# A gated four-layer transformer block on one core: the waits of an instruction written in another order

## The reference

```python
def reference(x, ctx, mask, g_xattn, g_ffn, ...):
    # layer 0: differential attention, 32 heads of 8; then 3 cycles of a coupling network
    x = x + tanh(g_xattn[0]) * L0_xattn(ln(x), ctx, ...)
    x = x + tanh(g_ffn[0])   * L0_ffn(ln(x), ...)
    # layer 1: 8 heads of 64, 512 keys, masked; then 2 shared + 8 routed experts, top 2, silu
    x = x + tanh(g_xattn[1]) * L1_xattn(ctx, ln(x), mask, ...)
    x = x + tanh(g_ffn[1])   * L1_ffn(ln(x), ...)
    # layer 2: 16 heads of 16; then attention of 16 heads of 8 and 8 experts, top 2, gelu
    x = x + tanh(g_xattn[2]) * L2_xattn(ln(x), ctx, ctx, ...)
    x = x + tanh(g_ffn[2])   * L2_ffn(ln(x), ...)
    # layer 3: one head of 256; then relu, 1024 hidden, weights and activations rounded to 8 bits
    x = x + tanh(g_xattn[3]) * L3_xattn(ln(x), ctx, ctx, ...)
    x = x + tanh(g_ffn[3])   * L3_ffn(ln(x), ...)
    return x
```

## Time and profile before

| what | value |
|---|---|
| median of three runs | 4452.66 us (4442.44 to 4463.31) |
| the profiled execution's own time | 4455.96 us |
| its span, first to last instruction | 4454.2 us |
| PE busy | 4098.3 us, 92% |
| PEld busy | 3191.7 us, 72% |
| DVE busy | 2944.5 us, 66% |
| ACT busy | 2054.1 us, 46% |
| mean granted TensorE clock | 0.953 of full speed |

### The profile page before, as it was taken

How to read it: one execution, slowest core, us unless ns; L and a number is a source line. 1 busy time by engine, 2 the same in 40 slices (tenths; PEclk the granted TensorE clock), 3 DMA queues, 4 the chain that set the end, 5 groups by cost and what they waited for, 6 DMA issues and landing times.

```text
span 4454.2 us, 73894 instructions
## 1 busy us (share of the span) xinstructions
PE 4098.3 (92%) x28256; PEld 3191.7 (72%) x28256; DVE 2944.5 (66%) x7812; ACT 2054.1 (46%) x3424; POOL 91.8 (2%) x180
## 2 busy tenths in 40 slices
PE   7898998989989899898999989899899998989988
PEld 4675876758767596675966759667696676867768
DVE  7666686676766767666675666757667576675754
ACT  4534455443553535535355352653535534355332
POOL 0000000000000000000000000000000000000000
PEclk8998999999999899998999999999999998999989
DMA  2010510103101030010300103001130011200012
GB/s 100 1 46 11 199 58 1 46 29 124 39 12 43 20 133 30 15 41 29 124 30 15 41 30 124 29 15 41 38 115 29 15 41 48 105 29 15 31 67 90
DMA packets 51769, 228.06 MB, mean 51 GB/s; under 512 B 4832, under 2 KB 21216, under 8 KB 31584
## 3 DMA queue, kind: packets, MB, share of 16 engines
q1 hardware_dynamic: 51424, 223.33, 13.9%
HBM read 202.34 MB, written 20.97 MB: 50 GB/s over the span
## 4 chain that ended last, share of the span: by engine, by line
PE 75%; DVE 14%; ACT 7%; issue 4%; DMA 0%; DVEq 0%; SPq 0%; ACTq 0%
PE w L578 18%; PE w L588 13%; PE w L824 8%; PE w L834 8%; PE o L713 5%; DVE mx L1248 4%; PE o L706 4%; PE w L562 4%; PE w L571 3%; PE w L629 3%; PE w L681 2%; PE w L646 2%; PE w L616 2%; PE w L725 1%; DVE nt L1189 1%
## 5 line engine op out<-in xcount | busy, mean ns | idle before, releaser
L1248 DVE TENSOR_REDUCE mx<-w 128x4 f32<-128x1024 f32 x512 | 602.0, 1221 | 178.7 <-PE w L629 171.7
L925 ACT ACTIVATE oth<-w,res 128x256 f32<-128x256 f32 x656 | 277.6, 471 | 562.7 <-PE w L824 463.6
L578 PE MATMUL w<-xnT,stream 128*128 128x256 f32 x1792 | 413.3, 383 | 1.8 <-ACT xnT L917 1.1
L578 PEld LDWEIGHTS w<-xnT,stream 128*128 128x128 f32 x1792 | 339.4, 191 | 51.0 <-DVE mx L1248 1.3
L824 PE MATMUL w<-qodd,va_hi 128*128 128x256 f32 x2048 | 356.4, 290 | 8.3 <-DVE x L1217 2.3
L824 PEld LDWEIGHTS w<-qodd,va_hi 128*128 128x128 f32 x2048 | 294.1, 194 | 19.0 <-issue 7.1
L980 ACT ACTIVATE pt_spread<-w 128x1024 f32<-128x1024 f32 x256 | 256.9, 1028 | 107.6 <-PE w L646 106.2
L1217 DVE SCALAR_TENSOR_TENSOR x<-w,gate,x 128x256 f32<-128x256 f32 x512 | 223.4, 478 | 110.8 <-PE w L834 93.0
L1507 DVE TENSOR_REDUCE mx<-w 128x2 f32<-128x1024 f32 x128 | 155.5, 1225 | 204.6 <-PE w L683 204.3
L629 PE MATMUL w<-ksp,qsp 32*128 32x256 f32 (+1 forms) x2048 | 237.2, 354 | 57.9 <-DVE mx L1248 22.3
L646 PE MATMUL w<-qsp,ksp 32*128 32x256 f32 (+1 forms) x2048 | 215.4, 334 | 54.4 <-DVE qsp L1267 25.2
(11 more groups left out here) (268 smaller groups left out, 8352.9 us busy)
## 6 DMA issues: line engine op xcount, KB each, us to landing
stream_lo<-split SPq DMA_DIRECT2D x56, 1024.0 KB, 4.8
va_hi<-split SPq DMA_DIRECT2D x56, 1024.0 KB, 6.9
stream<-in_moe_dram SPq DMA_DIRECT2D x80, 384.0 KB, 3.1
stream<-in_resident_dram SPq DMA_DIRECT2D x8, 2048.0 KB, 8.5
raw<-in_moe_dram SPq DMA_DIRECT2D x8, 1024.0 KB, 7.0
split<-va_hi SPq DMA_DIRECT2D x8, 1024.0 KB, 9.2
split<-stream_lo SPq DMA_DIRECT2D x8, 1024.0 KB, 11.1
stream<-in_resident_dram SPq DMA_DIRECT2D x8, 1024.0 KB, 4.7
```

What stands on the lines that cost most here:

```text
L578: mm = pe.matmul(w[:, col0 + j * T:col0 + j * T + T], weight[:, k, (m0 + j) * P:(m0 + j + 1) * P], act[:, k, :], start=(k == 0), stop=(k = ...
L925: h = act.activation(dst[:, c, :], w[:, c * T:(c + 1) * T], func, bias=bias[:, c:c + 1], **more)
L1248: dve.tensor_reduce(mx[s][:, :, 2 * v:2 * v + 2].rearrange("p t a -> p a t"), w[:, :].rearrange("p (a t k) -> p a t k", a=2, t=TT), AX_X, ...
```

## The change

Three kinds of edit, none of which moves, adds or removes a computing instruction or a DMA. Each engine's compute instructions stand in the same order as before.

1. On PE, `take` gets the data's waits as arguments and issues them ahead of the bank's, and it goes through the bank's last holders backwards. All PE steps that called `take` and then waited now pass their wait to it. In `values_by_exps` the wait for `s_P` is written first. So is that of some steps on ACT (`keep_item`, `ks`, `qs`, `l1.soft`, `f2.up`, `l3.k`) and DVE (`turn0`).
2. Waits that another wait contains are left out: `s_select` on PE in all but the first spread step, `s_xs` in all but the first expert, and on DVE the wait for `s_wfull` where it waits for ACT's result from the same bank anyway (`bank_of` in the place of `full`). In their place stands one `full` ahead of `l2.out` on DVE.
3. Event instructions fall from 2901 to 2751 on PE (those with two waits from 682 to 529) and from 1034 to 870 on DVE (those with two from 247 to 139). ACT keeps 1419.

```diff
@@ -547,9 +547,11 @@
-            def take(step, s, u=0):
-
-                for last in BANKS[step, s, u][2]:
+            def take(step, s, u=0, *needs):
+
+                for need in needs:
+                    pe.wait_ge(*need)
+                for last in BANKS[step, s, u][2][::-1]:
                     pe.wait_ge(*after(READ[last[0]], READER.get(last[0], last[0]), *last[1:]))
                 return bank_of(step, s, u)
@@ -604,9 +606,9 @@
                 elif what in ("ks", "qs"):
 
-                    w = take(st + "." + what, s, u)
-                    pe.wait_ge(*after("s_lo", st + "." + what[0], s))
-                    pe.wait_ge(s_select, 1)
+                    w = take(st + "." + what, s, u, after("s_lo", st + "." + what[0], s))
+                    if (st + "." + what, s, u) == FIRST_SPREAD:
+                        pe.wait_ge(s_select, 1)
@@ -632,14 +632,11 @@
                 elif what == "shift":
 
-                    w = take(st + ".shift", s, u)
-                    pe.wait_ge(*after("s_mp", st + ".peak", s))
+                    w = take(st + ".shift", s, u, after("s_mp", st + ".peak", s))
...
@@ -692,6 +684,7 @@
                 i = ITEM[st + ".pv", s, u - u % plan.units_per_item] - 1
+                pe.wait_ge(*after("s_P", st + ".exp", s, u))
                 if plan.item_starts(u) and i >= 2:
...
-                pe.wait_ge(*after("s_P", st + ".exp", s, u))
...
@@ -982,9 +953,9 @@
                 i = u // plan.units_per_item
+                act.wait_ge(*after("s_pv", plan.name + ".pv", s, u))
                 if i >= 4:
                     full(act, plan.name + ".back", s, i // 4 - 1)
-                act.wait_ge(*after("s_pv", plan.name + ".pv", s, u))
@@ -1223,7 +1195,7 @@
                     n = plan.chunks // 4
-                    w = full(dve, st + "." + what, s)
+                    w = bank_of(st + "." + what, s)
                     dve.wait_ge(*after("s_hi", st + "." + what, s))
...
```

More of the change, by code:

```diff
@@ L620, in spread_attention @@
                 elif what == "max":
[L622 to L625, removed]
+                    new = (after("s_qsp", st + ".qs", s, 1), after("s_ksp", st + ".ks", s, 1)) if u == 0 else ()
+                    w = take(st + ".max", s, u, *new)
                     for tt in range(TT):
@@ L652, in attention1 @@
                 if what in ("cT", "xT"):
-                    w = take("l1." + what, s)
+                    w = take("l1." + what, s, 0, after("s_xt", "l1.cln" if what == "cT" else "l1.ln", s))
                     pe.wait_ge(S["s_l1w"], 16 * (pass_of(s) + 1))
[L655 to L658, removed]
                     filled(transpose_features(w, qz[s][:, 0:2, :] if what == "cT" else xt[s]))
@@ L718, in back @@
             def back(plan, s, k):
-                w = take(plan.name + ".back", s, k)
-                pe.wait_ge(*after("s_oT", plan.name + ".pv", s, (4 * k + 4) * plan.units_per_item - 1))
+                w = take(plan.name + ".back", s, k, after("s_oT", plan.name + ".pv", s, (4 * k + 4) * plan.units_per_item - 1))
                 m = L1_DIM + 1 if plan is L1 else P
@@ L838, in layer_3 @@
             def layer_3(what, s):
-                w = take("l3." + what, s)
+                need = {"q": [("s_xnT", "l3.xT", s)], "max": [("s_qk3", "l3.q", s), ("s_qk3", "l3.k", s)], "exp": [("s_soft", "l3.soft", s)],
+                        "pv": [("s_P3", "l3.exp", s), ("s_v3", "l3.v", s)]}.get(what, [])
+                w = take("l3." + what, s, 0, *(after(*n) for n in need))
                 if what == "k":
@@ L885, in _ @@
                 elif what == "xT" and stage != "l1":
-                    w = take(step, s)
-                    pe.wait_ge(*after("s_xt", stage + ".ln", s))
+                    w = take(step, s, 0, after("s_xt", stage + ".ln", s))
                     filled(transpose_features(w, x0[s] if stage == "l0" else xt[s]))
@@ L1118, in _ @@
                     o = 0 if what == "q" else 2
+                    w = full(act, step, s)
                     if what == "k":
                         act.wait_ge(*after("s_pv", "f2.pv", s, F2.units - 1))
-                    biased(qk3[s][:, o:o + 2, :], full(act, step, s), W_["l3_b" + what], FC).then_inc(S["s_qk3"], 1)
+                    biased(qk3[s][:, o:o + 2, :], w, W_["l3_b" + what], FC).then_inc(S["s_qk3"], 1)
                 elif step == "l1.soft":
+                    act.wait_ge(*after("s_mx", "l1.max", s, u))
                     if u > 1:
@@ L1127, in _ @@
                             full(act, reader, s)
-                    act.wait_ge(*after("s_mx", "l1.max", s, u))
                     w = bank_of("l1.max", s, u)
@@ L1528, in _ @@
                 elif step == "l2.out":
+                    full(dve, "l2.out", s)
                     dve.wait_ge(*after("s_xb", "l2.bias", s))
```

69 lines of the change are left out of this document (23 added, 46 removed).

## The result

The changed kernel takes 4397.75 us (median of 4 runs, 4396.73 to 4398.10). The kernel before, run beside it, takes 4453.0. The ratio is 0.9876, with a 95% interval from 0.9852 to 0.9899: 1.24% or 55 us faster. The forecast was 4424 us, about half of that gain, and its range ended at 4400, 2.25 us above the time that came.

What follows compares the result with a forecast made beforehand. PE was taken to bound the kernel. Savings on the chain of 28.5 (PE), 2.0 (DVE) and 0.8 us (ACT) sum to 31.3; 0.9 of it, 28 us, gave 4424 us, range 4400 to 4446.

Steps and rivals of the forecast that it cites:

- How a wait is placed, and 0.10 for each event: At PE's waits: start 0.04, 0.14 or 0.25 us after the update, by where the last wait stands.
- The other size: At PE's waits: an estimate from the skill's page, about 62 ns off each wait, making PE's part 16 us.
- PE's sum: Issue pieces directly ahead of PE on the chain: 8.8 + 20.6 + 1.6 - 2.5 = 28.5 us saved.
- What arrives: Whole chain: 0.9 of the 31.3 us sum shows in the time, 28 us; bounds 0.3 and 1.6.
- The other ACT edits are off the chain: On ACT: edits beyond 13 late waits (0.8 us) are hidden behind PE's expert matmuls; uncovered, 0.05 to 0.09 us each.
- the only part that an order of waits can touch: Chain of waits: only "issue", from semaphore update to start of what waited, 4% or some 170 us, can change.
- The mean clock stays within 0.005: PE's clock in the changed profile: mean, 0.953 before, moves by no more than 0.005.
- Rival (c): PE's clock: fewer idle times lift its mean to 0.963, 25 us on top of the forecast, 4400 us; 7%.
- every idle time only shrinks by a tenth to a fifth: PE's idle times: argument against the clock's gain, since few idle times should fall out of what throttles it.
- (a): Chain moves to dense PE work or DVE's row maxima; 9 to 19 us gained, 4434 to 4444 us; 24%.
- (b): Waits still taken another way, or the last producer differs in most executions; 4453 us; 4%.
- (d): PE's work bunches differently, longer idle stretches form at DVE's maxima, mean clock falls; slower, 4475 us; 5%.

Runs made afterwards that it cites:

- PE's order: Kernel before with only PE's waits reordered and bank list reversed, no wait left out, ACT and DVE as before: 4413.38 us, ratio 0.9911.
- fillers: Changed kernel plus 523 matmuls of 128x128 with overwritten results, in 212 steps where PE waits for data: 4355.99 us, ratio 0.9779.
- one more event: Kernel before with one or two long-met waits added, so another event instruction stands behind the data's wait: 4481.55 us, ratio 1.0063.
- the fillers in the old order: Kernel before, waits in old order, plus the same 523 extra matmuls in the same 212 steps: 4394.30 us, ratio 0.9864.

## Why the prediction was wrong, step by step

- **How a wait is placed, and 0.10 for each event: right.** 0.25 became 0.04, 0.14 became 0.04, and an event added gave 0.10 more. The other size, 0.06 from the figure of the Trainium skill ("TensorE: Matmul & The Clock Gate", section "Wait — 56ns, not 53.3ns?"), is 0.04 too small at every such row here.
- **The counts: right.** Nearly no 0.25, 30 to 60 of 0.14 and over 250 of 0.04 were forecast, and the trace of PE's order has 1, 42 and 305; "issue" was to be 3% and is 3%. That the last producer is the same from one execution to the next held as well.
- **PE's sum: close.** 28.5 us were worked out. PE's order took 29 us off the chain's pieces and brought 24.4 at the same clock by the line, 19 by the traces.
- **DVE: right in sum, by two sizes that were not foreseen.** The one place in the earlier trace rows stood for all. On the chain of before 23 such places have three waits and gave 0.03 each, 18 have two and gave 0.07: 2.0 us, the forecast's figure, which was 28 times 0.07.
- **What arrives: 0.9 of 31.3, not refuted.** At the same clock came 30 to 39 us for the whole change, 29 to 32 in the pair with fillers, and some 5.6 of them are not in the sum. What is left, 24 to 33, is 0.8 to 1.1 of 31.3.
- **ACT: a step that failed.** "The other ACT edits are off the chain" took `l1.soft` along with the rest. I counted 0.8 us for ACT, 9.6 came for ACT and DVE at the same clock, and 5.6 of them are the table loads that an event instruction held back. That "issue" is "the only part that an order of waits can touch" failed with it: these 1.28 us stand in the trace as work of ACT. The row to look for was in the trace before: a table load whose releaser is the same DVE maximum as its exponential's.
- **"The mean clock stays within 0.005": the step that failed most.** It rose by 0.006 to 0.007, and PE's busy time, which was to stay, fell by 28.4 us. By the line over 63 runs the clock is worth 20 to 22 us, by the split of the two traces 27. Rival (c), at 7%, is what happened, on top of the forecast. That its 4400 lies 2.25 us from the time is partly luck: it had the clock at 0.963 and the price at 25 us per 0.01, against 0.959 and 32, and no table loads. What spoke against it, "every idle time only shrinks by a tenth to a fifth", is a quarter at the spread steps by its own rows (0.21 of 0.82 us), and was no measure of how often a stretch changes its clock: 68 us became faster and 41 slower in the same pair of traces.
- Rivals (a), (b) and (d) are refuted by the ratio.

Put together: the forecast's 28 us, 5.6 of table loads and 20 to 27 of clock make 54 to 61, where 55 to 62 came. The waits' part, 30 to 39 us, is shown by each part of the change alone; that the clock rises with the change by itself is shown by two sets of runs, and that idle stretches hold it down by the fillers. Not settled: how the reordered waits move the clock, and which stretches of idle time it answers to. The time at 1.2 GHz went from places all over the pass, and 28 us of idle time added in tenths of a us at the same waits left the clock where it was. A run with one idle stretch lengthened at a time would tell, and was not made.

## What to carry to other kernels

Write the wait that will come last first, so that it stands on the instruction, and price every place where it stood in an event instruction at 0.10 us per event; look beyond the main engine for a table load behind such an event. When a change removes idle time, forecast the clock as a term of its own, with a price taken from many runs of the unchanged kernel. Where PE must wait for data anyway, matmuls that only fill the stretch brought 61 us in the old order, about as much as the whole change of the waits (55 to 62), and both together 97 (in four of five runs); 57 matmuls more cost 5 us again.

## What was not expected of the hardware

- Latency by the place of the wait, medians over the late waits of the two traces: from the semaphore's update to PE's weight load 43 to 45 ns when the wait is the weight load's own, to the matmul 136 ns behind one event instruction (hundreds of waits each) and 246 behind two (some 60). On ACT 24 ns against 84 behind one.
- A table load of 1.28 us is held back by the event instructions of its activation but not by the activation's own wait, at all eight places here.
- 36 us between the fastest and the slowest run of one unchanged program follow its mean clock almost wholly (correlation -0.94, 2.7 us of scatter).
- 28 us slower without any change of the clock (one more event), and 61 us faster by matmuls that compute nothing, with the clock up by 0.024 (the fillers in the old order).
